# Three of the four loads of the next image wait for progress of the matrix engine, in a lambda-layer kernel

## The reference, cut to what matters

```
g   = group_norm(x, 32 groups)                       # needs the mean and variance of the whole image
h   = relu(bn1(conv1x1(g, 128)))
q   = bn(conv1x1(h, 64)); k = softmax(conv1x1(h, 16)); v = bn(conv1x1(h, 32))
pos = conv2d(v, emb, 15x15)                          # position lambdas, 16 per v channel
out = q . (k v^T) + q . pos                          # content part and position part, 4 heads
y   = x + relu(bn3(conv1x1(relu(bn2(out)), 512)) + g)
```

## Time and profile before

| | |
|---|---|
| time, median of 3 runs | 4826.06 us (4821.62 to 4826.49) |
| the profiled execution's own time | 4817.23 us |
| its span | 4815.5 us |
| PE busy | 4457.8 us, 93% |
| DVE busy | 2796.9 us, 58% |
| ACT busy | 2346.0 us, 49% |
| granted TensorE clock, mean | 0.949 |
| moved by the transfers | 1284.17 MB, 267 GB/s |

### The profile page before, as it was taken

How to read it: one execution, slowest core, us unless ns; L and a number is a source line. 1 busy time by engine, 2 the same in 40 slices (tenths; PEclk the granted TensorE clock), 3 DMA queues, 4 the chain that set the end, 5 groups by cost and what they waited for, 6 DMA issues and landing times.

```text
span 4815.5 us, 121009 instructions
## 1 busy us (share of the span) xinstructions
PE 4457.8 (93%) x49366; PEld 2717.4 (56%) x49366; DVE 2796.9 (58%) x4631; ACT 2346.0 (49%) x2880; POOL 967.9 (20%) x529
## 2 busy tenths in 40 slices
PE   4899999999999999999999999999999999999997
PEld 2555565655556655555555555555565556555555
DVE  3465555565655665656656556556566565566564
ACT  1455445554545454445544454544455444545453
POOL 0022211122201222202222112222122221112221
PEclk9899999999999999999999999999999999999998
DMA  3689778888778897788887788977888878889877
GB/s 96 214 278 308 239 265 279 275 296 277 249 272 266 282 309 250 254 274 288 281 291 243 265 266 276 307 251 254 272 292 281 288 245 275 270 273 305 263 248 250
DMA packets 537174, 1284.17 MB, mean 267 GB/s; under 512 B 43048, under 2 KB 225324, under 8 KB 528556
## 3 DMA queue, kind: packets, MB, share of 16 engines
q1 hardware_dynamic: 471276, 1017.22, 65.7%
q10 hardware_dynamic: 65472, 260.05, 14.7%
HBM read 844.79 MB, written 432.33 MB: 265 GB/s over the span
## 4 chain that ended last, share of the span: by engine, by line
PE 45%; SPq 18%; DMA 13%; issue 11%; DVE 6%; POOL 4%; ACT 2%; ACTq 0%; POOLq 0%; DVEq 0%
PE ring L527 16%; DMA X<-x_dram 11%; PE ring L653 10%; PE ring L508 7%; SPq L402 5%; PE ring L583 4%; SPq L360 4%; DVE st L884 3%; DMA q_parts<-region 3%; SPq L377 3%; POOL X L1189 2%; PE ring L534 2%; POOL region L1182 2%; SPq L378 2%; PE ring L539 2%
## 5 line engine op out<-in xcount | busy, mean ns | idle before, releaser
L702 ACT COPY region<-ring 126x1024 f32<-126x1024 f32 x1120 | 1102.9, 1016 | 948.0 <-PE ring L508 934.0
L583 PE MATMUL ring<-h,w3T 128*128 128x512 f32 x2048 | 937.7, 601 | 28.6 <-DVE X L1038 15.3
L653 PE MATMUL ring<-region,V 126*32 126x128 f32 x24576 | 889.2, 289 | 42.9 <-issue 42.7
L527 PE MATMUL ring<-X,w1e 128*128 128x512 f32 x2048 | 907.7, 596 | 3.2 <-DVE w1e L910 3.2
L508 PE MATMUL ring<-Qt,Ep 96*126 96x256 bf16 x5120 | 808.3, 298 | 103.9 <-DVE region L702 52.0
L653 PEld LDWEIGHTS ring<-region,V 126*32 126x32 f32 x24576 | 692.0, 116 | 223.3 <-issue 206.8
L702 DVE COPY region<-ring 126x1024 f32<-126x1024 f32 x416 | 507.5, 1220 | 496.6 <-PE ring L508 496.5
L508 PEld LDWEIGHTS ring<-Qt,Ep 96*126 96x126 bf16 x5120 | 598.9, 146 | 323.1 <-issue 139.4
L884 DVE BATCH_NORM_STATS2 st<-X 128x6 f32<-128x512 f32 x1024 | 624.8, 679 | 198.0 <-DMA X<-x_dram 197.9
L527 PEld LDWEIGHTS ring<-X,w1e 128*128 128x128 f32 x2048 | 384.5, 190 | 468.8 <-issue 465.5
L583 PEld LDWEIGHTS ring<-h,w3T 128*128 128x128 f32 x2048 | 370.0, 190 | 410.9 <-issue 371.5
(11 more groups left out here) (130 smaller groups left out, 3317.4 us busy)
## 6 DMA issues: line engine op xcount, KB each, us to landing
X<-x_dram SPq DMA_DIRECT2D x132, 2048.0 KB, 20.1
out_dram<-X SPq DMA_DIRECT2D x512, 512.0 KB, 8.0
X<-x_dram ACTq DMA_DIRECT2D x124, 2048.0 KB, 10.6
Qt<-q_parts SPq DMA_DIRECT2D x768, 128.0 KB, 3.1
V<-v_windows SPq DMA_DIRECT2D x96, 1024.0 KB, 10.5
lambda_sums<-S SPq DMA_DIRECT2D x64, 1024.0 KB, 5.0
h<-lambda_sums SPq DMA_DIRECT2D x256, 256.0 KB, 5.0
q_parts<-region SPq DMA_DIRECT2D x128, 256.0 KB, 4.2
```

The source lines that it names most:

```text
L527: last = nc.tensor.matmul(dst[:, hh * HALF:(hh + 1) * HALF], w1e[:, c, :], X[:, j, c, hh * HALF:(hh + 1) * HALF], start=(c == 0), stop=(c ...
L583: last = nc.tensor.matmul(dst[:, yb * HALF:(yb + 1) * HALF], w3T[:, t, :], src, start=True, stop=True)
L653: last = nc.tensor.matmul(bank_of(i)[c * DV:(c + 1) * DV, (g % 4) * P:(g % 4 + 1) * P], V[0:TROWS, VSLOT[t], xb, yb * DV:(yb + 1) * DV], W ...
L702: return engine_copy(dst, src)
```

## The change

SP's four loads of the next x no longer follow each other at once. The load of chunk 0 is as before. The loads of chunks 1, 2 and 3 wait, beside `out_done[j]`, until `w_full` has reached 48b + 8 + 8, + 14 and + 20: that is, until slot `w1.7` (made within the first unit, ahead of its last part), slot `w2.5` and slot `w3.3` are made. A semaphore `x_turn` is added to before and after each of these waits; nothing waits on it. The two loads of `load_v3` move from behind all four loads to between those of chunk 1 and chunk 2. In the last image, which loads no next x, the order stays.

```
+X_AFTER = [0, 8, 14, 20]
...
+        x_turn = sem("x_turn")
...
                     for j in range(NCH):
                         sp.wait_ge(out_done[j], b * (16 * CT) + HEAD)
+                        if j:
+                            sp.sem_inc(x_turn, 1)
+                            sp.wait_ge(w_full, b * (UNITS * NS) + NS + X_AFTER[j])
+                            sp.sem_inc(x_turn, 1)
                         load_x(b + 1, j)
-                load_v3(b)
+                        if j == 1:
+                            load_v3(b)
+                else:
+                    load_v3(b)
                 shuffle(b, 0)
```

## The result

The changed kernel takes 5022.72 us (median of 4, 5018.67 to 5026.41) beside 4823.84 us for the kernel before in the same runs: a ratio of 1.0415, 95% interval 1.0397 to 1.0433. It is 199 us slower, 6.4 us for each of 31 images. The forecast was 4882 us, in a range of 4822 to 4950: the direction and the start of the chain were right, the size was wrong by a factor of 3.4 (199 against 58 us), and the time lies above the range.

What follows compares the result with a forecast made beforehand. PE, 93% busy, was taken as the bound, tied to x landing, DVE's statistics and the sums' copy. 31 x 1.8 = 56 us on 4817.2 gave 4873, or 4882 us against the median; range 4822 to 4950.

Steps and rivals of the forecast that it cites:

- Steps 1, 3 and 4: On SP: added instructions, the issue of the v loads, and the waits of chunks 2 and 3 each cost nothing.
- Step 2: Chunk 1's wait on SP is hidden by the full queue: it still lands near 2085.2, cost 0.
- Step 5: In the DMA queue, the two v loads ahead of chunk 2 delay it 4.2 us, between 3.0 and 5.5.
- Step 6: On DVE, late chunk 2 adds a stall of 2.7 to 2.8 us, moving PE's second content part as much.
- Step 7: Behind PE's second content part, pauses absorb some delay; two thirds pass on: 1.8 us an image, 56 us.
- the factor of 0.65: Share of the second content part's delay taken to reach the stage's end: 0.65 x 2.8 = 1.8 us an image.
- A: Pauses behind PE's second content part absorb the delay, or nothing changes: 4826 us, within 10; chance 0.17.
- B: Faster, about 4772 us: PE's pauses named "issue" shrink by half as spaced loads sometimes empty the queue; chance 0.12.
- C: Much slower, about 4965 us: the stall lowers PE's clock at the second content part, costing 1.7 us more; chance 0.14.

Runs made afterwards that it cites:

- e1: The changed kernel with the two v loads put back behind chunk 3, the waits kept: 4818 us, ratio 0.9996.
- e2: The changed kernel without the waits and x_turn, the v loads still between chunks 1 and 2: 5027 us, ratio 1.0434.
- e3: The changed kernel with the two v loads as 128 rows with half the blocks each (other windows): 4819 us, ratio 1.0002.
- e12: e1 with chunks 2 and 3 waiting for slot w3.3 (X_AFTER 20): 4905 us, ratio 1.0173.
- e5: e1 with chunks 2 and 3 waiting for slot w3.5 (X_AFTER 22): 5033 us, ratio 1.0442.
- e6: e1 with chunks 2 and 3 waiting for slot w3.7 (X_AFTER 24): 5118 us, ratio 1.0620.
- e13: The kernel before with the two v loads, still last, in 128 rows (other windows): 4748 us, ratio 0.9850.
- e7: e3 with 126 rows instead of 128 in each v load: 4961 us, ratio 1.0296.
- e8: e3 with 64 rows and all eight blocks in each v load: 4998 us, ratio 1.0373.
- e14: e12 with the two v loads in 128 rows (other windows): 4879 us, ratio 1.0129.
- e9: The kernel before with chunks 0 and 1 of the next x issued ahead of the last eight stores: 4863 us, ratio 1.0076.
- e11: e2 with the two v loads one place later, between chunks 2 and 3: 5023 us, ratio 1.0411.

## Why the prediction was wrong in size

**Steps 1, 3 and 4 held.** The waits, their instructions and SP's hold-up in issuing cost nothing (e1, e2).

**Step 2 failed by a part.** "Chunk 1 still lands near 2085.2": it lands later (its statistics start at 29.5 instead of 27.4 us, so 2.1 us). It is ahead of the v loads in the queue, but its last pieces run beside their first, and what runs beside them is slowed. The row for it was at hand: chunk 3 of before was issued ahead of the v loads, and by the landing times of the profile it came 7.3 us behind chunk 2 (39.8 against 32.5 us) and not 5.1. I put that tail aside as hidden.

**Step 5 was the term mis-sized.** The v loads were priced at 4.2 us, between 3.0 and 5.5. S moved by 6.7 us and the play is 1.4, so they cost 8.1 us, and by its landing time chunk 2 is just that much later. The upper bound came from the six microseconds seen at the tail, where the slow stretch has chunk 3 in front and nothing of x behind it. In mid-stream it has a chunk on each side: 12 us at 216 GB/s. And the lower bound, from 128-row windows, was another kind of load: e3, with that kind, has 1.4 + 1.4 = 2.8 us.

**Step 6 held in kind.** The third wait appeared, 90 waits instead of 61, and 398 us instead of the 285 that I gave.

**Step 7 failed in sign.** "So the pauses behind it give some back": I read from three images that a late content part can end in time. But those images ran the same loads in the same order; their differences say nothing of a delay made by a load. In e12, e5 and e6, which keep the slow rows behind chunk 3, 1.4, 4.7 and 7.5 us at C give 2.9, 7.1 and 9.8 at E. The kernels that have nothing slow behind chunk 3 are to be held against e13 (E at 59.3): there 1.3 us (e3), 5.3 (e7), 6.3 (e8) and 6.6 (the changed kernel) give 2.1, 6.7, 8.0 and 8.8. So a delay costs 1.3 to 2.0 times itself, and in e14, with late chunks and the v loads behind them, 1.3 us even give 4.1. With nothing slow behind chunk 3, what was taken for slack isn't there: in e13 PE is idle 0.03 us from C to E, and the lower clock adds to the delay. In the changed kernel 2.1 us of it are given back, since the slow rows are gone from their old place: 8.8 - 2.1 = 6.7 us, 31 of them 208 us of span against 201 measured. With the factor of 0.65 the same delay would have made 133 us.

**The rivals.** A is refuted. B's condition didn't come about (the DMA share stays over 1.0 from 2158 to 2186 us), and the pauses named "issue" shrank by 22 us at the two lines of the earlier trace rows (13 us with those in front of the slots), not by 54. C was right in what it named: the second content part ran wholly or in part at 1.2 GHz in 23 of 31 images, PE's busy time rose by 60.7 us, 39.6 of it in the content part alone (215.7 against 176.1 us). I had given it 0.14 and kept it out of the forecast; it is nearly a third of the loss. The right answer was the forecast's mechanism with C's clock and twice the price.

**What stays open.** That the pauses named "issue" are PE's own instructions coming late was rival B's guess, and the traces bear it out: each of the 79 such pauses over 0.5 us in the kernel before ends 1.1 to 1.9 us after the end of a 16 KB packet of the instruction queue. Of PE's other waits 3% do, and of instants taken at random 7%. It is so for 98% or more of these pauses in every run. Why they come and go with the stream (107.6, 85.7, 78.6, 135.0 us at the same two lines in the kernel before, the changed one, e13 and e9) was not tested. And that the DMA engines' own partitions are the reason for the row shape was not seen directly.

## What to carry to other kernels

When a transfer is moved in a full queue, its own rate is not its price: look in the trace for the rate of everything beside it, at its old place as well, for a transfer that hides behind another may be costing already. Here two loads of 84 and 42 rows made the kernel 199 us slower when placed among loads that DVE waits for, and cost it 69 us where they stood. In full rows of 128 the 69 us were gone, and their place among the loads cost 2.1 us an image, 66 us in all (e3 against e13). And before a delay is discounted by the "slack" behind it, look at the clock: a stall can cost more than its own length.

## What the runs showed of the hardware that I had not expected

- A load of 1 MB in 1 KB pieces passed at 385 to 392 GB/s between 4 KB loads when it had 128 rows, and at 180 to 247 GB/s as 84 and 42 rows (rates of all that ran then); the 4 KB pieces beside it took 0.27 us on average in place of 0.16, and the 1 KB pieces 0.10 in place of 0.05, by the trace's records of the transfers. 64 rows gave 181 GB/s, less than half of 413.
- 126 rows, two short of 128, cost 142 us in this place (4961 beside 4818 us); 112 rows 77 us.
- Stalls of PE of 3.5 and 2.5 us were each followed by matmuls at a granted clock of 0.50, among them a content part of 3.61 us instead of 1.90; in e11, 115.5 of the 211.7 us by which the span grew were longer matmuls.
- Taking away 161 us of DVE's waits (e9) made the kernel some 40 us slower.
- Between the first and the last content part, every pause of PE over 0.5 us for which the profile shows no releaser ended 1.1 to 1.9 us after a 16 KB instruction packet had landed (79 of 79 in the kernel before, 56 of 56 in e13).
